# Cross-attention and mixture-of-experts block: three PSUM banks for the transposed scores, the small transposes moved into the score banks, scores two units further ahead

## The reference

```python
# x, ctx: (16, 128, 512); 8 heads of 16 features; the 512 columns are the positions
xn = layernorm(x)
qh, kh, vh = (t.reshape(16*8, 16, 512) for t in (xn, ctx, ctx))
qk = einsum('bdm,bdn->bmn', qh, kh) * 16 ** -0.5      # 512 x 512 scores a head
ret = einsum('bmn,bcn->bcm', softmax(qk), vh)
x = x + tanh(g_xattn) * ret.reshape(16, 128, 512)
x = x + tanh(g_ffn) * moe(layernorm(x))               # 16 experts, top 4, one shared
```

## Time and profile before

| | |
|---|---|
| median of 3 runs | 1304.0 us (1292.27 to 1304.32) |
| the profiled execution, own time | 1302.71 us |
| its span | 1300.6 us |
| mean granted TensorE clock | 0.98 of full |
| busy in the span: PE, DVE, ACT, POOL | 91%, 59%, 40%, 44% |
| matmuls of the attention, first T to last T | 36.6 to 485.3 us |

### The profile page before, as it was taken

One profiled execution on the slowest core, in us unless ns is written; L12 is line 12 of the kernel. 1 busy time (PEld: TensorE's weight loads), 2 busy tenths in 40 slices (PEclk: granted clock), 3 DMA queues, 4 the chain that ended last, 5 costly groups with the idle time before them and its releaser, 6 DMA issues.

```text
span 1300.6 us, 21683 instructions
## 1 busy us (share of the span) xinstructions
PE 1179.1 (91%) x6020; PEld 773.9 (60%) x6021; DVE 767.1 (59%) x1194; ACT 517.1 (40%) x1040; POOL 567.9 (44%) x490
## 2 busy tenths in 40 slices
PE   2888888888888988999979999999999999999996
PEld 0333333333333335887858777777777777788885
DVE  5888877888888842873334343333333333337877
ACT  1677666677667771111101123333333333321110
POOL 2144333333443225034854435537355473317753
PEclk9999888999999998999979999999999999999999
DMA  9365655556656425956451434544644545424655
GB/s 241 119 172 162 191 160 156 152 146 171 179 157 173 108 67 191 393 189 221 170 193 41 162 120 146 179 176 152 203 150 157 193 154 200 151 67 114 171 170 177
DMA packets 104814, 214.57 MB, mean 165 GB/s; under 512 B 12352, under 2 KB 17472, under 8 KB 104768
## 3 DMA queue, kind: packets, MB, share of 16 engines
q1 hardware_dynamic: 85408, 152.08, 38.4%
q0 software_dynamic: 18016, 61.88, 14.6%
q10 hardware_dynamic: 1344, 0.04, 0.1%
HBM read 117.48 MB, written 91.75 MB: 161 GB/s over the span
## 4 chain that ended last, share of the span: by engine, by line
PE 58%; issue 2%; DVE 1%; DVEq 0%; ACT 0%
PE score_ps L131 18%; PE score_ps L1488 17%; PE d_ps L1443 9%; PE d_ps L1511 8%; PE score_ps L1469 3%; PE d_ps L1500 1%; PE d_ps L1396 1%; DVE y_all L1290 1%; DVE y_all L1278 0%; DVEq L154 0%; PE d_ps L1419 0%; PE score_ps L1405 0%; PE d_ps L1412 0%; DVE hid L1360 0%; DVE th L1355 0%
## 5 line engine op out<-in xcount | busy, mean ns | idle before, releaser
L584 DVE TENSOR_REDUCE maxima<-score_ps 128x2 f32<-128x1024 f32 x256 | 308.3, 1222 | 49.0 <-PE score_ps L688 38.5
L537 ACT ACTIVATE probs<-sb_ps 128x512 f32<-128x512 f32 x512 | 278.0, 595 | 111.9 <-PE sb_ps L702 106.5
L131 PE MATMUL score_ps<-yn_t,w_split 128*128 128x512 f32 x1056 | 256.3, 400 | 11.6 <-issue 10.7
L131 PEld LDWEIGHTS score_ps<-yn_t,w_split 128*128 128x128 f32 x1056 | 199.9, 190 | 63.6 <-issue 14.8
L1488 PE MATMUL score_ps<-w_split,x_split 128*128 x948 | 236.7, 398 | 0.0
L1488 PEld LDWEIGHTS score_ps<-w_split,x_split 128*128 128x128 f32 x948 | 172.3, 188 | 33.3
L1007 POOL CAST w_split<-w_raw 128x1024 fp32r<-128x1024 f32 x63 | 66.0, 1047 | 259.7 <-POOLq L1077 149.1
L1009 POOL TENSOR_TENSOR w_split<-w_raw,w_split 128x1024 fp32r<-128x1024 f32 x63 | 152.0, 2412 | 5.1
L713 PE MATMUL o_ps<-probs,v_t 128*32 128x512 f32 x1024 | 141.9, 628 | 0.0
L1443 PE MATMUL d_ps<-w_split,h_split 128*128 128x512 f32 x528 | 125.0, 391 | 2.0 <-issue 2.0
L1511 PE MATMUL d_ps<-w_split,h_rows 128*128 x474 | 120.4, 389 | 0.0
(11 more groups left out here) (142 smaller groups left out, 1378.9 us busy)
## 6 DMA issues: line engine op xcount, KB each, us to landing
xs_dram<-zero SPq DMA_DIRECT2D x1, 20224.0 KB, 58.7
stage<-xs_dram SPq DMA_DIRECT2D x79, 256.0 KB, 2.8
res_dram<-stage SPq DMA_DIRECT2D x79, 256.0 KB, 2.0
k_dram<-k_hi SPq DMA_DIRECT2D x16, 512.0 KB, 2.8
q_dram<-q_hi SPq DMA_DIRECT2D x16, 512.0 KB, 3.9
w_raw<-in_L_ffn_w_gate_dram POOLq DMA_DIRECT2D x16, 512.0 KB
w_raw<-in_L_ffn_w_up_dram POOLq DMA_DIRECT2D x16, 512.0 KB
w_raw<-in_L_ffn_w_down_dram POOLq DMA_DIRECT2D x16, 512.0 KB
```

The source lines that it names most:

```text
L131: mm = pe.matmul(dst[i], w[:, k, f * P:(f + 1) * P], self.yn_t[:, b, k, t * self.SPAN:(t + 1) * self.SPAN], start=(n == 0), stop=(n == 3 * ...
L537: act.activation(probs[:, c % 2, head(j)[2], :], sb_ps[:, j % 2, :], ACT.Exp, scale=SCALE).then_inc(exp_done, 1)
L584: dve.tensor_reduce(maxima[q % 2][:, :].rearrange("p (h u) -> p u h", u=8)[:, u, :], sa_ps[:, u % 2, :, :], AX_X, ALU.max).then_inc(max_do ...
```

## The change

- `sb_ps` grows from two banks to three, and `m_ps` is gone. T number e of a group uses bank e % 3 for e < 8 and (e+1) % 3 from e = 8 on. The place left out at e = 8 is M's (bank 2). B and N, now one step "L" at the end of a slot, use bank 2 as well, between a slot's e = 13 and the next slot's e = 2.
- O writes one bank of a pair of `score_ps`, as a ninth turn among the eight units: the turns are 6, 7, 0, 1, O, 2, 3, 4, 5. O therefore waits until unit 0 is reduced, and unit 3 waits until `normalise` has read O.
- The scores run two units further ahead: slot g computes units 6 and 7 of group g+1 and units 0 to 5 of group g+2. Slot 0 makes up the difference with 10 units.
- DVE's order in a slot: unit 6, unit 7, split, statistics, unit 0, the aggregate of the statistics, unit 1, normalise, units 2 to 5.
- The residual addition leaves DVE: ACT scales the turned batch into a new tile `back`, POOL adds it to `x_res`. The additions of the layernorm's epsilon (L567, L624) go from DVE to POOL. POOL splits N's result (`split_yn`) one slot later; for batch 14 that is right behind the last slot and ahead of the expert weights.

```diff
-        sb_ps = ps("sb_ps", [P, 2, D])
+        sb_ps = ps("sb_ps", [P, 3, D])
         o_ps = ps("o_ps", [P, D])
-        m_ps = ps("m_ps", [P, D])
...
+        PLACE = {6: 0, 7: 1, 0: 2, 1: 3, 2: 5, 3: 6, 4: 7, 5: 8}
+        OUTPUTS, VALUES, LAST = 4, 8, 17
...
+            return (q - (1 if u >= 6 else 2) + PLACE[u]) % 2
+
+        def pair_of_outputs(s):
+            return (s.q + OUTPUTS) % 2
+
+        def bank_of_score(e):
+            return e % 3 if e < VALUES else (e + 1) % 3
...
+            def residual(b, j, n):
+
+                pool.wait_ge(scaled_done, b + 1)
+                pool.wait_ge(res_loaded[j], 16 * n + 16)
+                pool.tensor_tensor(x_res[j][:, :], back[:, :], x_res[j][:, :], ALU.add).then_inc(y_done, 1)
...
             slots(pool, slot)
+            split_yn(B - 2)
...
             def slot(s):
                 for c in range(KC):
-                    if c == 2 and has_late(s):
-                        copy_yn(batch_late(s))
-                    if c == 3 and s.before(NG - 1):
-                        values_and_maxima((s.q + 1) % 4, s.g + 1, s.r)
+                    if c == 2 and s.before(NG - 1):
+                        values_and_maxima((s.q + 1) % 4, s.g + 1, s.r, VALUES % 3)
...
+                if has_back(s):
+                    scale_back(batch_back(s), LAST % 3)
+                if has_late(s):
+                    copy_yn(batch_late(s))
...
+                if s.before(NG - 1):
+                    unit(q1, g + 1, 6)
+                    unit(q1, g + 1, 7)
+                    split_maxima(q1, g + 1)
                 if prepared(s):
                     statistics(q // 2, s.r + 1)
                     dve.wait_ge(bn_done, 2 * s.r + q // 2 + 3)
-                if s.before(NG - 1):
-                    unit(q1, g + 1, 4)
+                if has_late(s):
+                    last_statistics(batch_late(s), 1 if q == 1 else 0)
+                    dve.wait_ge(bn2_done, batch_late(s) + 1)
+                if s.before(NG - 2):
+                    unit(q2, g + 2, 0)
...
-            ORDER = (("TSTSTSTSV", "TSTSOTSTSV", "TSTSMTSTSV", "TSTSBTSTSV"),
-                     ("TSTSSSTTV", "TSTSOTSTSVN", "TSTSMTSTSV", "TSTSSSTTV"))
+            ORDER = ("TSTSTSTSV", "TSTSTSTSOV", "MTSTSTSTSV", "TSTSTSTSVL")
+            FIRST_ORDER = ("TSSTSSTSSTSSV",) + ORDER[1:]
...
                         elif step == "O" and s.at_least(1):
-
-                            if q % 2 == 1 and s.at_least(3):
-                                pe.wait_ge(y_done, 2 * r + q // 2)
+                            if s.before(NG - 2):
+                                pe.wait_ge(max_done, 8 * g + 17)
                             else:
-                                pe.wait_ge(vt_done, g + 1)
-                            outputs_t(g - 1)
+                                pe.wait_ge(max_done, 8 * NG - 1 if g == NG - 2 else 8 * NG)
+                            outputs_t(g - 1, sa_ps[:, pair_of_outputs(s), 0, :])
```

More of the change, by code:

```diff
@@ L202, in gated_block @@
         mean_var = [sb(f"mean_var{i}", [P, 2]) for i in range(2)]
-        var_eps = [sb(f"var_eps{i}", [P, 1]) for i in range(2)]
+        back = sb("back", [P, D])
+        var_eps = sb("var_eps", [P, 1])
+        eps = sb("eps", [P, 1])
         rstd = [sb(f"rstd{i}", [P, 1]) for i in range(2)]
@@ L288, in fix_rows, with pair_of_unit, units_of @@
             eng.memset(k_stack[i][:, :, :].bitcast(F32), -1.0).then_inc(fixed_rows[i], 1)
+        PLACE = {6: 0, 7: 1, 0: 2, 1: 3, 2: 5, 3: 6, 4: 7, 5: 8}
+        OUTPUTS, VALUES, LAST = 4, 8, 17
+        def pair_of_unit(q, g, u):
+            if isinstance(g, int) and g < 2:
+                return u % 2
+            return (q - (1 if u >= 6 else 2) + PLACE[u]) % 2
[3 more added lines that the diff above has]
+            return e % 3 if e < VALUES else (e + 1) % 3
+        def units_of(s):
+            one, two = ((s.q + n) % 4 for n in (1, 2))
+            found = []
+            if s.known() and s.g == 0:
+                found += [(1, 1, 0, u) for u in (4, 5)]
+            if s.before(NG - 1):
+                found += [(one, s.g + 1, s.r + (s.q + 1) // 4, u) for u in (6, 7)]
+            if s.before(NG - 2):
+                found += [(two, s.g + 2, s.r + (s.q + 2) // 4, u) for u in range(6)]
+            return found
         def head(j):
@@ L595, in split_maxima, with normalise @@
                 dve.tensor_tensor(lo, whole_max, hi, ALU.subtract).then_inc(mlo_done, 1)
-            def normalise(q, g, b):
-                view = m_ps[:, :].rearrange("p (k h e) -> p k h e", k=KC, h=HG)
+            def normalise(q, g, b, bank):
+                view = bank.rearrange("p (k h e) -> p k h e", k=KC, h=HG)
                 dve.wait_ge(ot_done, g + 1)
@@ L632, in slot @@
                 q1, q2 = (q + 1) % 4, (q + 2) % 4
-                if has_late(s):
-                    residual(batch_late(s), 1 if q == 1 else 0, s.r - 1 if q == 1 else s.r)
-                    dve.wait_ge(bn2_done, batch_late(s) + 1)
+                if s.known() and g == 0:
+                    unit(1, 1, 4)
+                    unit(1, 1, 5)
+                if s.before(NG - 1):
+                    unit(q1, g + 1, 6)
+                    unit(q1, g + 1, 7)
+                    split_maxima(q1, g + 1)
                 if prepared(s):
```

194 lines of the change are left out of this document (103 added, 91 removed).

## The result

| | before | after |
|---|---|---|
| median of 20 runs each, on the same chip | 1302.1 us (1292.27 to 1316.34) | 1294.1 us (1288.70 to 1301.91) |
| ratio, with its 95% interval | | 0.9936 [0.9917, 0.9954] |
| the profiled execution, own time | 1302.71 us | 1292.20 us |
| mean granted TensorE clock | 0.98 | 0.98 |

The changed kernel is faster by 0.6%, some 8 us. The forecast was 1310 us, 0.5% slower. The time lies inside the range, but it went the other way, by more than the measurement leaves open.

The account below looks back on a forecast made before the run. PE was taken as the bound only between its pauses (for M's split and for exponentials to free banks), DVE close behind. 1302.7 + 1 (slots) + 3.5 (ends) = 1307, with 3 for clock falls 1310 us; range 1284 to 1334.

Parts of the forecast that it names:

- +1 in the slots: Attention slots 1 to 29: 14.1 us each replaces a mean of 14.07, 29 x 0.03 = +1 us.
- The wait only changes place: Attention: O's wait for unit 0's reduction eats what three banks gave; the forecast itself, 1303 to 1317 us, chance 0.50.
- Slot of 14.1 us: Rolled attention loop: O starts at 5.81 us, next slot at 14.1; bounds 14.1 to 14.55 by the split's length.
- The walk: One attention slot timed step by step on DVE and PE from its first T, giving O at 5.81, slot 14.1 us.
- Ends, +3.5, bounds 0 to +6: First and last slots and work behind them: slot 0 +1, slots 30 and 31 -1, behind the last +2.3 and +1.2.
- Clock, +3 for one or two falls: Attention: one to two falls of PE's clock at 2.8 us each, +3; bounds none to 28 us.
- Rival (2), more falls: Attention: PE's pause before O in every slot makes the clock fall 8 to 12 times, 1329 to 1341 us; chance 0.17.
- Rival (3), chain shorter: DVE's chain ahead of O is shorter than walked: slot 13.6 us, no falls, 1293 us, from 1284 to 1302; chance 0.15.
- Rival (4), 12.6 us a slot: Attention: O hardly waits and the change does what it can, slot 12.6 us, 1263 us; chance 0.10.

Follow-up runs that it names:

- e1: Kernel before with 12 idle semaphore increments on PE just ahead of the expert tile loop: 1276.8 us against 1286.3, ratio 0.9938, tile loop 387.9 us.
- e15: Kernel before with 12 idle semaphore increments at the very start of PE's program, ahead of the attention: tile loop 387.7 us.
- e3: Changed kernel with DVE's statistics moved from ahead of unit 0 to between unit 0 and unit 1: 1245.8 us, 0.9694 of the kernel before.
- e6: Changed kernel, unchanged, run again on another chip: 1274.2 us, 0.9927 of the kernel before.
- e4: Changed kernel with both the split of the maxima and the statistics moved behind unit 0 on DVE: 1245.1 us, 0.9689 of the kernel before.
- e7: Changed kernel, three banks kept, but T waits for the exponential two before it as with two: 1343.2 to 1346.8 us in three of six executions, ratio 1.0477.
- e16: Kernel before with 40 idle semaphore increments on DVE ahead of its tile loop, none on PE: tile loop 396.8 us.

## Why the prediction was wrong

**The step that failed** is one that it never wrote down as a term: that outside the attention nothing changes. All of the sum is about the attention and its two ends. The tile loop's 7.6 us came from a shift of 12 places in PE's program, and 12 idle instructions in the kernel before give the same ratio (e1) and the same loop (e15). Nothing in the trace of before said "place", but a row that said "pause" was there: 12.2 us of issue at L1469, in one tile of every two.

**Without the loop it would still have been too high.** To the router it expected +1 in the slots, +3.5 at the ends and +3 for the clock, 7.5 us; the two pairs of profiles show -1.7 and -3.9. The term that was mis-sized is the one for the slots: +1 us for 29 of them, -9.8 us measured over 30. Point by point:

- *The wait only changes place*: right. M's wait gone, O's there, 29 times, 31.7 us; split of 0.17 and 0.17 us with POOL idle, statistics right behind it, O at 5.72 us against 5.81 walked. That this chain holds the slot is shown by e3: without its 0.89 us of statistics the slot is 12.94 us.
- *Slot of 14.1 us*: the mechanism was right and the size off, 13.78 measured. The walk was 0.09 late at O, 0.06 from O's V to M (1.00, since M's extra wait costs nothing) and 0.17 from M to the next slot (6.48 instead of 6.65). Exponentials follow each other after 0.47 to 0.49 us and not 0.56: the four exponentials behind M took 2.01 us, where the group of the earlier trace rows took 2.27. That group had waited for PE, so it most likely measured PE's spacing and not ACT's. From a unit's second S to its reduction it is 0.46 and not 0.57 (273.36 to 273.82). 0.3 us a slot is small, but times 29 it is 9 us, more than the whole forecast of the change.

```profile
281.46 2.01 ACT L592 ACTIVATE probs<-sb_ps 128x512 f32<-128x512 f32 x4
```

- *Ends, +3.5, bounds 0 to +6*: undersized, about +8 in the first profile, +0.2 at slot 0 and +7.9 behind slot 30. The POOL split ahead of the weights cost what was said, +2.35. Two falls of the clock there were no term: a V of 1.94 us ahead of the pause of 3.05 us, and +2.4 in the 12 matmuls behind it. They don't follow from the pause alone: in e6 the same pause had matmuls of 4.61 us behind it, in e4 of 3.07. 1.45 of the 7.9 is only M's earlier place in its slot. e6, the same kernel again, had 40.7 us instead of 43.6.
- *Clock, +3 for one or two falls*: the three slots with a fall lost 6.0 us, twice the term. But they were compared with a mean of 14.07 that held five falls and 10.5 us of them. The forecast counted the old falls in its base and new ones on top; it should have set 14.0 against 13.8 and falls against falls.
- *Rival (2), more falls*: did not happen, though every slot pauses 1.0 to 1.25 us before O. e7 shows that the danger is real: pauses of 0.4 to 0.6 us, some five a slot, brought the mean clock to 0.91 and nearly doubled the loss (72.5 us for 37).
- *Rival (3), chain shorter*, gave 1293 us, next to the 1294.1 measured, but for another reason: its 14 us in the slots were 9.8, the ends took back 8.1, and the loop gave the rest. The number is right by luck.
- *Rival (4), 12.6 us a slot*: its argument against itself, four steps ahead of unit 0 on DVE, was the right one. With two of them gone (e4) the slot is 12.96 us and the time 0.9689 of before, some 1262 us on the first chip's scale (0.9689 x 1302.1); it had given 1263. Here too the loop has its part, 395.6 less 388.4 us; without it, 1269, so this number too is met partly by luck.

**What stays open.** The loop's place counts modulo 256, and the pauses sit at the first transpose of every second tile: in the 78 groups of transposes before, 36 of the 39 pauses stand at the first tile of a turn, which is the head of the loop's body, right behind the jump back. Which instruction of the loop must not stand at which place of a block is not shown: in the old place an edge of a block may fall on one of the loop's ends, but a row that shows the fetch itself was not found, and that the pause is a fetch is not shown. Also open is what makes the clock fall in one slot with a pause of 1.24 us before O (262.62) and not in its neighbour with 1.23 (248.76), and behind a pause of 3.04 us in e6 and not in e4.

## What to carry to other kernels

When a transpose is given a turn among the scores' banks, it inherits all that stands ahead of its turn on the engine that frees the bank: put only the releasing reductions there, and the statistics behind them (2.4% of the time more, where the change brought 0.6, most of it by the loop's new place). Split a profile into stages before you credit a change: a loop whose code is the same can run 2% slower or faster because the code ahead of it grew by one instruction, and the control for it is the kernel before with as many idle instructions. Read an engine's pitch only from a group that did not wait inside, and compare slots with a fall of the clock with others of their kind.

## What the runs showed of the hardware

- The place of a rolled loop in PE's program sets its pace, and it comes back after 256 instructions: 395.6 us at the original place (396.8 in e16), 394.6 at 256 behind it, 387.5 to 390.1 at the others tried. That is 2% of the loop.
- Semaphore increments in a row on PE cost about 0.1 us each: 52 of them 5.6 us, 32 of them 2.6, 256 of them 25.8.
- Here many pauses of half a microsecond were worse for the clock than one of 1.2 us a slot: a mean of 0.91 in e7 against 0.98 after and 1.00 with the pauses of 0.3 us in e4.
- The granted clock does not show the lower level of the first slots: it reads 1.00 from the start, while T takes 0.79 us instead of 0.50 until 46.6 us before and 56.7 us in e4.
- A fall in the attention costs less than the PE time that it halves: some 6.8 us at the lower level made a slot 2.3 to 2.8 us longer, where 3.4 would be the estimate for a PE that never waits.
